# Layer 2's attention: one order of steps per engine, ctx a head pair later, its copy on ScalarE

## What is computed

```
x = x + _L2_attn_ref(_layernorm(x), ...)

q = jnp.einsum('bsd,hpd->bhsp', x, q_w) + q_b      # 16 heads of 64
k = jnp.einsum('bsd,hpd->bhsp', x, k_w) + k_b
v = jnp.einsum('bsd,hpd->bhsp', x, v_w) + v_b
scores = jnp.einsum('bhqp,bhkp->bhqk', q, k) / jnp.sqrt(jnp.float32(P))
attn = jax.nn.softmax(scores, axis=2)              # over the queries
ctx = jnp.einsum('bhqk,bhkp->bqhp', attn, v)
out = ctx.reshape(...) @ l_w.T + l_b
```

## Time and profile before

| | us |
|---|---|
| median of 3 runs | 1525.72 |
| the three runs | 1525.72, 1523.18, 1525.88 |
| the profiled execution | 1523.27 |
| its span, first to last instruction | 1521.4 |
| TensorE busy (matmuls) | 1411.6 |
| TensorE weight loads busy | 643.1 |
| VectorE busy | 1243.0 |
| ScalarE busy | 1078.1 |
| GpSimd busy | 281.5 |

### The profile page before, as it was taken

One profiled execution on the slowest core, in us unless ns is written; L12 is line 12 of the kernel. 1 busy time (PEld: TensorE's weight loads), 2 busy tenths in 40 slices (PEclk: granted clock), 3 DMA queues, 4 the chain that ended last, 5 costly groups with the idle time before them and its releaser, 6 DMA issues.

```text
span 1521.4 us, 23190 instructions
## 1 busy us (share of the span) xinstructions
PE 1411.6 (93%) x8387; PEld 643.1 (42%) x8387; DVE 1243.0 (82%) x2660; ACT 1078.1 (71%) x1990; POOL 281.5 (19%) x238
## 2 busy tenths in 40 slices
PE   6568999999989978999999999999999988999995
PEld 3442222222258756233333333333333335566784
DVE  7776777777378888888888898888898887999994
ACT  4537999999857622777777787777777875887544
POOL 3100000000013341111111111111111112234454
PEclk9789999999989979999999999999999999999997
DMA  3045555555310101000000000000000000000000
GB/s 98 4 119 128 150 149 152 146 145 152 112 53 2 72 1 70 1 1 1 1 1 1 0 1 1 1 1 1 1 1 1 1 28 1 1 8 8 8 14 22
DMA packets 43602, 63.11 MB, mean 41 GB/s; under 512 B 5344, under 2 KB 25056, under 8 KB 43104
## 3 DMA queue, kind: packets, MB, share of 16 engines
q1 hardware_dynamic: 43488, 61.62, 14.6%
HBM read 54.27 MB, written 7.34 MB: 40 GB/s over the span
## 4 chain that ended last, share of the span: by engine, by line
PE 67%; DVE 15%; issue 8%; POOL 5%; ACT 3%; DMA 1%; POOLq 0%; SPq 0%; DVEq 0%; ACTq 0%
PE ps L2007 13%; PE ps L1998 10%; PE ps L277 7%; PE ps L554 7%; PE ps L1977 5%; PE ps L2017 4%; PE ps L1987 3%; DVE p6ac L2495 2%; PE ps L563 2%; PE ps L700 2%; PE ps L2434 2%; POOL WA L2187 1%; PE ps L2397 1%; PE ps L191 1%; POOL WA L2191 1%
## 5 line engine op out<-in xcount | busy, mean ns | idle before, releaser
L2094 ACT ACTIVATE p4E<-ps,p4mx,p4sc 128x512 f32<-128x512 f32 x512 | 392.6, 773 | 138.9 <-DVE p4mx L2053 138.9
L2051 DVE TENSOR_REDUCE p4mx<-ps 128x2 f32<-128x1024 f32 x256 | 312.7, 1221 | 65.1 <-PE ps L1998 62.8
L2007 PE MATMUL ps<-p4E,p4vn 128*64 128x512 f32 x1024 | 248.6, 606 | 8.1 <-POOL p4vn L2112 8.0
L1998 PE MATMUL ps<-p4T 64*128 64x512 f16 x1536 | 199.6, 379 | 3.9 <-ACT p4E L2094 3.2
L2112 POOL TENSOR_TENSOR p4vn<-p4v,p4zs 128x512 f32<-128x512 f32 x64 | 66.7, 1042 | 494.0 <-DVE p4zs L2056 494.0
L167 POOL TENSOR_TENSOR rs<-rs,cst 128x4 f32<-128x4 f32 x58 | 63.1, 1088 | 479.5 <-DVE rs L161 479.2
L277 PE MATMUL ps<-p1R,p1w1s 128*128 128x512 bf16 x512 | 144.9, 385 | 3.3 <-ACT xn L286 2.5
L286 ACT ACTIVATE p1g<-ps,WB 128x1024 f32<-128x1024 f32 x128 | 137.6, 1134 | 13.5 <-PE ps L277 12.8
L586 DVE SCALAR_TENSOR_TENSOR p1Pb<-ps,WB,p1sh 128x512 f32<-128x512 f32 x128 | 94.7, 748 | 56.6 <-PE ps L554 56.5
L554 PE MATMUL ps<-p1g,WB 128*32 128x512 f32 x512 | 136.3, 612 | 0.0
L554 PE MATMUL ps<-xn,WB 128*32 128x512 f32 x256 | 135.4, 612 | 0.3 <-DVE p1Pb L586 0.3
(11 more groups left out here) (349 smaller groups left out, 2483.9 us busy)
## 6 DMA issues: line engine op xcount, KB each, us to landing
p1sh<-gscr SPq DMA_DIRECT2D x128, 256.0 KB
p1R<-tscr SPq DMA_DIRECT2D x64, 128.0 KB, 4.8
tscr<-p1tp SPq DMA_DIRECT2D x24, 128.0 KB, 2.3
WA<-in_w SPq DMA_DIRECT2D x1, 2632.0 KB, 9.8
WB<-in_w SPq DMA_DIRECT2D x1, 2560.0 KB, 8.8
X<-in_x SPq DMA_DIRECT2D x8, 256.0 KB, 5.5
gscr<-p1gT SPq DMA_DIRECT2D x8, 256.0 KB, 4.8
out<-X SPq DMA_DIRECT2D x8, 256.0 KB, 2.3
```

What stands on the lines that cost most here:

```text
L1998: y = p.e.matmul(ps[:, at + hh, :], t[rows, q, 128 * j:128 * j + 128], t[rows, 2 + r, :], start=o == 0, stop=o == 2)
L2007: t = p.e.matmul(ps[64 * hh:64 * hh + 64, 7, :], vn[n % 2][:, j, 64 * hh:64 * hh + 64], E[2 * (n % 2) + hh][:, j, :], start=j == 0, stop=j ...
L2051: v.e.tensor_reduce(m, ps[:, at:at + 2, :], AX, ALU.max).then_inc(v.own.h, v.one())
L2094: a.e.activation(self.E[2 * i + hh][:, j, :], ps[:, at + hh, :], ACT.Exp, bias=self.mx[i][:, j, hh:hh + 1], scale=pre.sc[:, 1, 0:1], accum ...
```

## The change

- Each engine gets an order of its own, written out as a string of letters (a table `ORDER`, a letter for a kind of step, the steps of one kind always in their natural order). `steps` lists what there is of each kind. Steps that one name covered before have names of their own now: **rstd** for GpSimd's part of stats, **add** for VectorE's part of project.
- ctx of unit n stands beside the scores of n+2 and no longer of n+1. For that E has six tiles instead of four (three units), and the exponentials of n wait for ctx of n-3 instead of n-2.
- ctx has no bank of its own any more: kq, vproj, ctx, turn and squares go round over the banks 4, 5 and 7, and `released` waits for the use three back.
- ctx out is a copy by ScalarE, not by VectorE.

The tables differ from the old order in many places besides. A line of the table and the core of the rest:

```diff
-        self.E = [loc(f"E{i}", [128, 4, 512]) for i in range(4)]
+        self.E = [loc(f"E{i}", [128, 4, 512]) for i in range(6)]
...
-        uses = list(self.uses())
-        self.bank = {u: 4 + i % 2 for i, u in enumerate(uses)}
-        self.last = {u: uses[i - 2] for i, u in enumerate(uses) if i > 1}
+        uses = [u for what, x in self.order("tensor") for u in self.banks(what, x)]
+        self.bank = {u: (4, 5, 7)[i % 3] for i, u in enumerate(uses)}
+        self.last = {u: uses[i - 3] for i, u in enumerate(uses) if i > 2}
...
+    KINDS = {
+        "a": "vproj", "b": "kq", "c": "score", "d": "ctx", "e": "project", "f": "turn", "g": "ahead", "h": "stats", "i": "low parts",
+        "j": "rows", "k": "values", "l": "turned", "m": "add", "n": "largest", "o": "ctx out", "p": "bias", "q": "rstd", "r": "load",
+    }
+    ORDER = {
+        "tensor": (
+            "aaaaaaaabbbbccabbacccbccbcdcdcabcbecdcdcabcbedccdcacbbecdcdcabcbecdcdcabcbecdcdcfacbecbdcdcabcbecdcdcabcbecdcd"
...
+        "vector": (
+            "hhaaaaaaaahhiiijiccajjjhahccihhcckihcjcjjjickicachhciickhcacjjjjhhhccikiccahhciickhhcacjjjcijckihcacjjjcjihcki"
...
+    def order(self, engine):
+
+        left = {kind: iter(among) for kind, among in self.steps().items()}
+        for letter in self.ORDER[engine]:
+            kind = self.KINDS[letter]
+            yield kind, next(left[kind])
...
+        elif what == "ctx":
+            p.wait_ge(k.sem("cx"), x + 1)
...
             elif what == "ctx":
                 n, half = x
-                p.wait_ge(k.sem("cx"), n)
                 p.wait_ge(k.sem("vn"), n + 1)
                 p.wait_ge(k.sem("E"), 8 * n + 8)
+                if not half:
+                    self.released(p, ("ctx", n))
...
-            elif what == "ctx out":
-                v.wait_ge(k.sem("ctx"), x + 1)
-                v.wait_ge(k.sem("y4"), x - 1)
-                v.e.tensor_copy(self.cx[x % 2][:, :], ps[:, 7, :]).then_inc(k.sem("cx").h, 1)
...
-                a.wait_ge(k.sem("ctx"), n - 1)
+                a.wait_ge(k.sem("ctx"), n - 2)
...
+            elif what == "ctx out":
+                a.wait_ge(k.sem("ctx"), x + 1)
+                a.wait_ge(k.sem("y4"), x - 1)
+                a.e.copy(self.cx[x % 2][:, :], ps[:, self.bank["ctx", x], :]).then_inc(k.sem("cx").h, 1)
```

More of the change, by code:

```diff
@@ L1874, in __init__ @@
         self.cx = [loc(f"cx{i}", [128, 512]) for i in range(2)]
-        uses = list(self.uses())
-        self.bank = {u: 4 + i % 2 for i, u in enumerate(uses)}
-        self.last = {u: uses[i - 2] for i, u in enumerate(uses) if i > 1}
+        uses = [u for what, x in self.order("tensor") for u in self.banks(what, x)]
+        self.bank = {u: (4, 5, 7)[i % 3] for i, u in enumerate(uses)}
+        self.last = {u: uses[i - 3] for i, u in enumerate(uses) if i > 2}
     PARTS = ((0, 0), (1, 0), (0, 1))
[L1881 to L1927, removed]
-            late = n - 12 if 12 <= n < 33 else n - 27 if 48 <= n < 62 else None
-            if late is not None:
-                yield "ahead", late
-                if late < 10 and late % 2:
-                    yield "largest", late // 2
-            if n == 8:
-                yield "load", 5
-            if n == 62:
-                yield "load", 6
@@ new lines, in steps @@
+    def steps(self):
+        units, later = range(8 * NB), range(2, NB)
+        every = {"kq": [(n, c) for n in units for c in range(2)], "score": [(n, j) for n in units for j in range(4)],
+                 "ctx": [(n, half) for n in units for half in range(2)], "vproj": [(b, i) for b in range(NB) for i in range(8)],
+                 "ahead": range(35), "largest": range(5), "bias": range(NB), "load": range(5, 7),
+                 "stats": [(b, i) for b in later for i in range(4)], "rows": [(b, i) for b in later for i in range(4)]}
+        every["low parts"] = every["kq"]
+        every |= {what: units for what in ("values", "ctx out", "project")}
+        every |= {what: later for what in ("rstd", "turn", "turned")}
+        every["add"] = range(NB)
+        return every
@@ new lines, in order, with banks @@
+    def order(self, engine):
[3 more added lines that the diff above has]
+            yield kind, next(left[kind])
+    def banks(self, what, x):
+        if what in ("kq", "vproj"):
+            return [(what, x)]
+        if what == "ctx" and not x[1]:
+            return [(what, x[0])]
+        if what == "turn":
+            return [(what, 8 + x)]
+        if what == "ahead" and x < 10 and x % 2:
+            return [("squares", x // 2)]
+        if what == "ahead" and x in (25, 30):
+            return [("turn", 16 + (x - 25) // 5)]
+        return []
@@ L1950, in released, with evacuated @@
     def released(self, p, use):
+        if use in self.last:
+            self.evacuated(p, self.last[use])
+    def evacuated(self, p, use):
         k = self.k
[L1953 to L1955 removed]
+        what, x = use
         if what == "kq":
@@ L2028, in vector @@
         ahead = self.low.vector(v)
-        for what, x in self.order():
+        for what, x in self.order("vector"):
             if what == "low parts":
@@ L2080, in scalar @@
         ahead = self.low.scalar(a, self.bank)
-        for what, x in self.order():
+        for what, x in self.order("scalar"):
             if what == "kq":
@@ L2104, in gpsimd @@
         ahead = self.low.gpsimd(g)
-        for what, x in self.order():
+        for what, x in self.order("gpsimd"):
             if what == "values":
@@ L2124, in sync @@
         k = self.k
-        for what, x in self.order():
+        for what, x in self.order("sync"):
             if what == "load":
```

54 lines of the change are left out of this document (32 added, 22 removed).

## The result

| | before | after |
|---|---|---|
| median, us | 1524.45 (4 runs) | 1504.28 (4 runs) |
| profiled execution, its span | 1523.27, 1521.4 | 1503.48, 1501.6 |
| first matmul of the stage to the last projection | 669.5 | 648.6 |

The changed kernel takes 0.9867 of the time of before (95% interval 0.985 to 0.9884): 20 us less, where 7.3 were forecast. Of the 19.8 us between the spans the stage gave 20.9; it starts 0.7 later and what follows it is 0.4 longer.

The account below looks back on a forecast made before the run. TensorE was taken as the bound, issuing back to back. Work -2.3, start +2.6, middle -5.7 and tail -1.9 sum to -7.3 us: 1523.3 becomes 1516.0, put at 1517 us for the median; range 1512 to 1524.

Parts of the forecast that it names:

- TensorE's work: Whole stage: 508 changes of tile form instead of 561, so 645.9 us of work instead of 648.2, -2.3 us.
- waits up to score 9.3: TensorE's waits from the stage's first matmul to score 9.3: 10.7 us against 8.1 before, +2.6 us.
- waits in the middle: TensorE's waits from score 9.3 to score 63.3: 2 us (1 to 5) instead of 7.7, -5.7 us.
- waits behind score 63.3: TensorE's waits from score 63.3 to the last projection: 3.5 us against 5.4 before, -1.9 us.
- The price of a half of ctx: TensorE's products with the values: a half costs 1.87, or 1.92 us ahead of a score, with no wait in it.
- The price of a projection: TensorE's output projection costs 1.09 us, also when it stands beside kq.
- Pairings free: TensorE's vproj to kq and kq to project, same tile form: 0.65 us from start to start, not 0.75.
- rival (c): TensorE's vproj to kq and kq to project are not free: +9.7 on 1516, so 1526 us; 4%.
- The middle: Score 9.3 to 63.3: the wait for vn goes, ScalarE's copy costs nothing while 0.6 us of slack holds; -5.7 us.
- The start: Up to score 9.3: VectorE, full with early LayerNorm statistics and rows, delays that score to 702.0 from 699.8; +2.6 us.
- The tail: After score 63.3: output projection 62 fills the gap before the last ctx, the clock perhaps staying at 2.4 GHz; -1.9 us.
- Rival (b): ScalarE's queue: the copy waits for ctx and delays exponentials; slower from 0.7 us late, 1535 us at 0.9; 8%.

## Why the prediction was wrong, step by step

The stage was forecast at 662.1 us and took 648.6. The missing 13.5 us by the terms of the sum:

| term | forecast | measured |
|---|---|---|
| TensorE's work | 645.9 | 634.6 |
| waits up to score 9.3 | 10.7 | 10.1 |
| waits in the middle | 2 | 1.4 |
| waits behind score 63.3 | 3.5 | 2.5 |

The waits up to score 9.3 are the 105.8 us to its start at 700.43, less the work; the work is the forecast's with the two prices below put right, and the waits of the other two rows are what then remains of the time between the starts.

Against before, by the same prices put right, the gain has two halves; this is an estimate from the starts of the two traces. TensorE's work fell by 10.4 us (53 changes of form less and 51 projections, 0.10 each). Its waits fell by some 10: 9 in the middle and 3 at the end less, 1 to 2 at the start more.

- **The price of a half of ctx (the step that failed, 6.2 us).** "They add up to 10.04 us for a head pair, and nothing in them is a wait." That was not so. Of the two halves in the earlier trace rows one took 1.87 and one 1.91, and I took the second for the price ahead of a score. The wait was in my own numbers: further on I read that exponentials end at 707.88 and score 2 starts at 708.02, took the 0.14 between them for TensorE's delay, and called the limit "exactly met". A limit that is exactly met in every pair is a wait. The run with the shorter maximum shows 1.87 there, and the trace of before itself had it, 12 times among the 64 halves ahead of a score. 124 halves x 0.05 = 6.2 us.
- **The price of a projection (the second step that failed, 5.1 us).** I kept 1.09 beside kq, because the earlier trace rows has no other. Behind a group of its own form it is 0.99, 51 times in after, once read as 0.98, and in the two kernels of before with a projection behind kq or vproj. 51 x 0.10. A change of form ahead of it costs the projection 0.10 on top of the 0.10 that the group ahead shows.
- **Pairings free: right.** vproj to kq (45 times) and kq to projection (51 times) take 0.65 or 0.66; rival (c) is out. The Trainium skill (TensorEngine Tiling (Array Packing), Key Properties) says that a change of tiling mode drains TensorE; the trace fits this and gives the price, 0.10 us each, so that 0.65 becomes 0.75, but does not show what TensorE does in it.
- **The middle: right**, and the copy too (0.58 against 0.57). But my reason, that vn has 8 us more time, does not suffice: with ctx a pair later in the common order the wait for vn went and one for exponentials came. That in after the scores stand apart fits this, and was not tried alone.
- **The start: right** to 1.6 us at score 9.3 (700.43 against 702.0), not for the reason given, so by luck. I took the full VectorE for the cause, but spreading its steps changed nothing, and half the maximum took away a quarter of the waits. 1.3 of the 10.1 us are the half clock behind 613.72. What makes the rest is open; the largest, 3.05 us at 613.72, is a score's wait for exponentials, with no ctx yet to put between.
- **The tail: right in kind, 1 us better.** The clock stayed at 2.4 GHz: both halves of ctx in 3.65 us.
- **The bank: costed at nothing**, and worth 2 to 4 us when it is alone, 2.0 of them at the start.
- **Rival (b)**, ScalarE's queue, is out: the copy ends 0.43 before it would hold anything up.

What each part is worth depends on the others. Alone, ctx a pair later gives 0, the copy 0, the bank 2 to 4 us, and TensorE's cheaper neighbourhoods cost 5 to 19 us; together 20. The runs show two links: with vproj ahead of the projection TensorE's order needs an order of VectorE's own (18 to 24 us), and the copy is worth 7 to 9 us once VectorE's first 27 pairs are as full as in the changed kernel. How much the later ctx adds to these two stays open.

## What to carry to other kernels

Price a group by its shortest distance to the next in the trace, not by the one at the place in question; where the same pair of groups has two distances, look up when the other engine ended, and take the difference for a wait if that end is just ahead of each start. A cheaper order on the engine that is the bound did not pay here in any common order that I tried, and paid in the one try where VectorE took its steps in an order of its own. In two of the common orders, moving one step on TensorE brought a kq closer behind a score, and the maximum of that score, which VectorE takes ahead of the step that frees kq's bank, no longer fitted in between. So before such a move is costed, walk what stands between the freed resource and its waiter on every engine.
